# One-hots by group, one product for both fields: the placing step of a routed feed-forward on Trainium2

## What is computed

```python
def _L1_ffn_ref(x, Wr, br, ln_g, ln_b, W1, b1, W2, b2):
    TOP_K = 2
    xt = x.reshape(N, D)
    logits = xt @ Wr + br
    probs = jax.nn.softmax(logits, axis=-1)
    top_p, top_idx = jax.lax.top_k(probs, TOP_K)
    weights = top_p / top_p.sum(axis=-1, keepdims=True)
    ...
    xn = (xt - mu) * jax.lax.rsqrt(var + LN_EPS)
    xe = xn[None, :, :] * ln_g[:, None, :] + ln_b[:, None, :]
    h = jax.nn.gelu(jnp.einsum('end,edh->enh', xe, W1) + b1[:, None, :], approximate=False)
    y = jnp.einsum('enh,ehd->end', h, W2) + b2[:, None, :]
    ...
    out = (weights[:, :, None] * sel).sum(axis=1)
```

## Time and profile before

| | |
|---|---|
| median of 3 runs | 3544.34 us (3541.79 to 3544.54) |
| the profiled execution, its own time | 3536.91 us |
| span of the core in it | 3535.1 us |
| mean granted TensorE clock | 0.873 of full speed |
| TensorE busy | 2639.2 us (75%) in 15311 instructions |
| VectorE busy | 2619.7 us (74%) in 6603 |
| ScalarE busy | 1007.9 us (29%) in 2073 |
| GpSimd busy | 2179.5 us (62%) in 2147 |

### The profile page before, as it was taken

One profiled execution on the slowest core, in us unless ns is written; L12 is line 12 of the kernel. 1 busy time (PEld: TensorE's weight loads), 2 busy tenths in 40 slices (PEclk: granted clock), 3 DMA queues, 4 the chain that ended last, 5 costly groups with the idle time before them and its releaser, 6 DMA issues. The chain is left out here.

```text
span 3535.1 us, 55789 instructions
## 1 busy us (share of the span) xinstructions
PE 2639.2 (75%) x15311; PEld 2236.0 (63%) x15311; DVE 2619.7 (74%) x6603; ACT 1007.9 (29%) x2073; POOL 2179.5 (62%) x2147
## 2 busy tenths in 40 slices
PE   6888466666666665899956776777677569999997
PEld 4777354444444444789945555555555369999997
DVE  6999566666666666969967777777777778888886
ACT  0021000000000002545501111111111268888886
POOL 0455577777777774345567777777777235555554
PEclk9999677788788777999978888888888789999999
DMA  3011433333333332001133333333333447777775
GB/s 98 10 43 33 121 105 106 105 105 105 105 106 105 106 105 66 1 3 37 45 99 113 111 112 113 112 112 112 111 113 112 130 145 209 214 213 210 209 213 131
DMA packets 164679, 389.01 MB, mean 110 GB/s; under 512 B 46378, under 2 KB 95602, under 8 KB 151019
## 3 DMA queue, kind: packets, MB, share of 16 engines
q0 software_dynamic: 99072, 233.49, 24.5%
q1 hardware_dynamic: 65387, 152.94, 13.3%
HBM read 343.97 MB, written 42.98 MB: 109 GB/s over the span
## 5 line engine op out<-in xcount | busy, mean ns | idle before, releaser
L1081 POOL DMA_INDIRECT g_got<-table,e_source x1568 | 1492.0, 952 | 505.9 <-issue 458.2
L1174 PE MATMUL psum<-g_got,g_route 128*128 x3328 | 1082.0, 483 | 649.5 <-DMA g_got<-table,e_source 266.0
L1174 PEld LDWEIGHTS psum<-g_got,g_route 128*128 128x128 f32 x3328 | 760.4, 239 | 892.0 <-issue 766.9
L1107 DVE TENSOR_TENSOR A<-A,psum 128x256 f32 x1664 | 698.8, 420 | 525.7 <-PE psum L1174 347.4
L1090 DVE TENSOR_SCALAR g_route<-columns,e_local,e_weight 128x128 f32<-128x128 f32 x1664 | 471.1, 362 | 17.5 <-issue 12.5
L368 POOL DMA_INDIRECT records<-rec,place x120 | 149.6, 1247 | 220.4 <-ACT rec L580 122.2
L142 PE MATMUL psum<-e_xt_hi,e_w_hi 128*128 128x256 f32 x832 | 238.9, 287 | 34.3 <-DVE e_w_lo L1973 25.8
L1582 POOL TENSOR_TENSOR f_ht_lo<-f_ht,f_ht_hi 128x512 fp32r<-128x512 f32 x100 | 133.9, 1343 | 185.7 <-ACT f_ht_hi L1531 180.2
L142 PE MATMUL psum<-e_w_hi,e_ht_hi 128*128 128x256 f32 x832 | 237.5, 285 | 3.1 <-DVE e_w_lo L1981 3.1
L1860 POOL DMA_INDIRECT out<-e_y,e_homes x104 | 198.9, 1913 | 63.4 <-POOL e_homes L1856 47.6
L144 PE MATMUL psum<-e_xt_hi,e_w_lo 128*128 128x256 f32 x832 | 233.6, 281 | 0.0
(11 more groups left out here) (420 smaller groups left out, 5147.7 us busy)
## 6 DMA issues: line engine op xcount, KB each, us to landing
e_w<-in_m_w SPq DMA_DIRECT2D x104, 1024.0 KB, 5.3
g_got<-table,e_source POOLq DMA_INDIRECT x1568, 2.8
expert_table<-g_normal SPq DMA_DIRECT2D x52, 128.0 KB
table<-xn SPq DMA_DIRECT2D x49, 128.0 KB, 1.7
X<-in_x SPq DMA_DIRECT2D x1, 6144.0 KB
table<-f_ring SPq DMA_DIRECT2D x24, 256.0 KB, 2.1
out<-X SPq DMA_DIRECT2D x1, 6144.0 KB
f_w<-in_f_w SPq DMA_DIRECT2D x2, 1024.0 KB, 6.8
```

Of the source, the lines that this page charges most:

```text
L1081: pool.indirect_dma_start(got[:, c % RING, :], None, rows, bass.IndirectOffsetOnAxis(ap=source[:, c:c + 1].bitcast(U32), axis=0)).then_inc ...
L1107: dve.tensor_tensor(to, to, sums_of(c), ALU.add).then_inc(added, 1)
L1174: ins = pe.matmul(sums_of(c), route[:, c % (GB + GSEM), :], row(got, at[j % GSEM]), start=True, stop=True)
```

## The change

The one-hots of a group are written by one tensor_tensor each, from bf16 operands: the numbers 0 to 127, each repeated 14 times (`numbers_b`), against the 14 slots' `slot_hi` or `slot_lo`, now bf16 too. So the slots stand innermost: `is_hi` is [112, 14] and `is_lo` [128, 14] in a partition, where they were [14, 112] and [14, 128]. ScalarE reads `is_hi` across that order and writes `fields` as [14 slots, 2 fields, 112], each operation's output with its innermost dimension contiguous. One product of 224 columns for each slot then takes both fields, and its stationary operand, `is_lo[:, u, :, c]`, is read in steps of 14 elements. The two fields' sums, now side by side in bank 5, are added by VectorE before `node_of`.

Further: TensorE makes the totals of the experts with seven accumulating products of 112 columns, ahead of its others, and VectorE reduces their 14 x 8 numbers. `pick` is compared with the numbers less 8 (`lower`, made by GpSimd) instead of having 8 added. GpSimd waits for `node_of` behind its reading of the number of pairs instead of ahead of it. VectorE waits, before it writes the first low part of w1, until GpSimd has copied the second pair of nodes. `dense` and `second` share memory with `others` and `picked`.

```diff
-            dense, second = early("dense", [P, NT, NE]), early("second", [P, NT, NE])
+            dense, second = others, picked
...
-            is_lo = early("is_lo", [P, 2, 2 * GROUP, P], BF16)
-            is_hi = early("is_hi", [P, 2, 2 * GROUP, SC], BF16)
-            fields = here("fields", [P, 2, 2, 2 * GROUP, SC], BF16)
+            is_lo = early("is_lo", [P, 2, P, 2 * GROUP], BF16)
+            is_hi = early("is_hi", [P, 2, SC, 2 * GROUP], BF16)
+            fields = here("fields", [P, 2, 2 * GROUP, 2, SC], BF16)
+            numbers_b = early("numbers_b", [P, P, 2 * GROUP], BF16)
...
+                        if isinstance(m, int) and m == 0:
+                            pool.wait_ge(chosen, NODES)
                         wait(pool, x_ready, m - 1)
...
+                pool.tensor_scalar(lower[:], columns[:, 0:NE], -float(NE), None, ALU.add).then_inc(prepared, 1)
+                pool.tensor_copy(ones_b[:], ones[:]).then_inc(prepared, 1)
                 pool.tensor_copy(before_b[:], before[:]).then_inc(prepared, 1)
-                pool.tensor_copy(ones_b[:], ones[:]).then_inc(prepared, 1)
-                pool.tensor_copy(columns_b[:], columns[:]).then_inc(prepared, 1)
+                pool.tensor_copy(numbers_b[:], columns[:].unsqueeze(2).to_broadcast([P, P, 2 * GROUP])).then_inc(prepared, 1)
...
+                for q in range(GROUPS):
+                    ins = pe.matmul(psum[:, 6, 0:2 * GROUP * NE], ones_b[:], flat[:, q * 2 * GROUP * NE:(q + 1) * 2 * GROUP * NE],
+                                    start=q == 0, stop=q == GROUPS - 1)
+                ins.then_inc(ranked, 1)
...
-                    pe.wait_ge(fields_ready, 8 * g + 1)
-                    for c in range(2 * GROUP):
-                        pe.matmul(psum[:, 5, 0:SC], is_lo[:, u, c, :], fields[:, u, 0, c, :], start=opens and c == 0, stop=False)
                     for i in range(GROUP):
                         pe.wait_ge(fields_ready, 8 * g + (2 + i))
                         for c in (2 * i, 2 * i + 1):
-                            ins = pe.matmul(psum[:, 5, 0:SC], is_lo[:, u, c, :], fields[:, u, 1, c, :], start=False,
-                                            stop=closes and c == 2 * GROUP - 1)
+                            ins = pe.matmul(psum[:, 5, 0:2 * SC], is_lo[:, u, :, c], fields[:, u, c, :, :].rearrange("p f h -> p (f h)"),
+                                            start=opens and c == 0, stop=closes and c == 2 * GROUP - 1)
...
                         if isinstance(m, int) and m == 0:
+                            dve.wait_ge(nodes_ready, 2)
                             low_of_w1(m, u)
...
-                    s(dve.tensor_scalar(pick[:], pick[:], float(NE), None, ALU.add))
-                    s(dve.tensor_tensor(hot[:, :, k, :], numbers, wide(pick[:]), ALU.is_equal))
+                    s(dve.tensor_tensor(hot[:, :, k, :], lower[:].unsqueeze(1).to_broadcast([P, NT, NE]), wide(pick[:]), ALU.is_equal))
...
-                dve.tensor_reduce(count[:], hot[:].rearrange("p t k e -> p e (t k)"), AX.X, ALU.add).then_inc(chosen, 1)
...
+                s(dve.tensor_reduce(count[:], psum[:, 6, 0:2 * GROUP * NE].rearrange("p (c e) -> p e c", e=NE), AX.X, ALU.add))
...
-                    high_hots(g, u)
-                    for c in range(2 * GROUP):
-                        ins = dve.tensor_scalar(is_lo[:, u, c, :], columns_b[:], slot_lo[:, bass.ds(g * (2 * GROUP) + c, 1)], None, ALU.is_equal)
-                    ins.then_inc(hots_ready, 1)
+                    for to, of, wide, done in ((is_hi, slot_hi, SC, is_hi_ready), (is_lo, slot_lo, P, hots_ready)):
+                        dve.tensor_tensor(to[:, u, :, :], numbers_b[:, 0:wide, :],
+                                          of[:, bass.ts(g, 2 * GROUP)].unsqueeze(1).to_broadcast([P, wide, 2 * GROUP]),
+                                          ALU.is_equal).then_inc(done, 1)
...
-                dve.tensor_scalar(node_of[:], psum[:, 5, 0:SC], -1.0, 0.0, ALU.add, ALU.max).then_inc(chosen, 1)
+                s(dve.tensor_copy(pad[:], psum[:, 5, 0:SC]))
+                s(dve.tensor_tensor(number[:], pad[:], psum[:, 5, SC:2 * SC], ALU.add))
+                dve.tensor_scalar(node_of[:], number[:], -1.0, 0.0, ALU.add, ALU.max).then_inc(chosen, 1)
...
-                    act.activation(fields[:, u, 0, :, :].rearrange("p c h -> p (c h)"), is_hi[:, u, :, :].rearrange("p c h -> p (c h)"),
+                    act.activation(fields[:, u, :, 0, :], is_hi[:, u, :, :].rearrange("p h c -> p c h"),
                                    ACT.Copy, scale=part_1[:, 0:1]).then_inc(fields_ready, 1)
                     for i in range(GROUP):
-                        act.activation(fields[:, u, 1, 2 * i:2 * i + 2, :].rearrange("p c h -> p (c h)"),
-                                       is_hi[:, u, 2 * i:2 * i + 2, :].rearrange("p c h -> p (c h)"),
+                        act.activation(fields[:, u, 2 * i:2 * i + 2, 1, :], is_hi[:, u, :, 2 * i:2 * i + 2].rearrange("p h c -> p c h"),
                                        ACT.Copy, scale=float(P * (g * GROUP + i))).then_inc(fields_ready, 1)
```

More of the change, by code:

```diff
@@ L1767, in build @@
             slot_f, slot, slot_part = early("slot_f", [P, C]), early("slot", [P, C], I32), early("slot_part", [P, C], I32)
-            slot_lo, slot_hi = early("slot_lo", [P, C]), early("slot_hi", [P, C])
-            is_lo = early("is_lo", [P, 2, 2 * GROUP, P], BF16)
-            is_hi = early("is_hi", [P, 2, 2 * GROUP, SC], BF16)
-            fields = here("fields", [P, 2, 2, 2 * GROUP, SC], BF16)
-            columns_b, before_b, ones_b = (early(what, [P, P], BF16) for what in ("columns_b", "before_b", "ones_b"))
+            slot_lo, slot_hi = early("slot_lo", [P, C], BF16), early("slot_hi", [P, C], BF16)
+            is_lo = early("is_lo", [P, 2, P, 2 * GROUP], BF16)
+            is_hi = early("is_hi", [P, 2, SC, 2 * GROUP], BF16)
+            fields = here("fields", [P, 2, 2 * GROUP, 2, SC], BF16)
+            numbers_b = early("numbers_b", [P, P, 2 * GROUP], BF16)
+            before_b, ones_b = (early(what, [P, P], BF16) for what in ("before_b", "ones_b"))
+            lower = early("lower", [P, NE])
+            number = at[:].rearrange("p c e -> p (c e)")[:, 0:SC]
             part_1, pad, past_end = early("part_1", [P, 1]), early("pad", [P, SC]), early("past_end", [P, 2])
@@ L1941, in _ @@
                 halves = [flat[:, h * NT * NE:(h + 1) * NT * NE] for h in range(2)]
-                pe.wait_ge(prepared, 8)
+                pe.wait_ge(prepared, 9)
                 pe.wait_ge(chosen, CHOICES)
+                for q in range(GROUPS):
+                    ins = pe.matmul(psum[:, 6, 0:2 * GROUP * NE], ones_b[:], flat[:, q * 2 * GROUP * NE:(q + 1) * 2 * GROUP * NE],
+                                    start=q == 0, stop=q == GROUPS - 1)
+                ins.then_inc(ranked, 1)
                 for h in range(2):
                     pe.matmul(psum[:, 3 + h, 0:NT * NE], ones_b[:], halves[h], start=True, stop=True).then_inc(ranked, 1)
-                pe.wait_ge(chosen, COUNT)
-                pe.matmul(psum[:, 6, 0:NE], ones[:], count[:], start=True, stop=True).then_inc(ranked, 1)
                 for h in range(2):
@@ L2043, in _ @@
                 dve.tensor_tensor(behind[:], top[:, :, 1], top[:, :, 0], ALU.subtract).then_inc(chosen, 1)
-                dve.tensor_reduce(count[:], hot[:].rearrange("p t k e -> p e (t k)"), AX.X, ALU.add).then_inc(chosen, 1)
-                for h in range(2):
-                    dve.wait_ge(ranked, h + 1)
-                    s(dve.tensor_copy(sums[:, :, 1 + h * NT:1 + (h + 1) * NT],
-                                      psum[:, 3 + h, 0:NT * NE].rearrange("p (c e) -> p e c", e=NE)))
                 dve.wait_ge(ranked, TOTALLED)
-                s(dve.tensor_scalar(ntile_i[:], psum[:, 6, 0:NE], float(MT - 1), None, ALU.add))
+                s(dve.tensor_reduce(count[:], psum[:, 6, 0:2 * GROUP * NE].rearrange("p (c e) -> p e c", e=NE), AX.X, ALU.add))
+                s(dve.tensor_scalar(ntile_i[:], count[:], float(MT - 1), None, ALU.add))
                 s(dve.tensor_scalar(ntile_i[:], ntile_i[:], 8, None, ALU.logical_shift_right))
@@ L2055, in _ @@
                 s(dve.tensor_scalar(sums[:, :, 0], first[:], float(MT), None, ALU.mult))
-                dve.wait_ge(prepared, 8)
+                for h in range(2):
+                    dve.wait_ge(ranked, COUNTED + h)
+                    s(dve.tensor_copy(sums[:, :, 1 + h * NT:1 + (h + 1) * NT],
+                                      psum[:, 3 + h, 0:NT * NE].rearrange("p (c e) -> p e c", e=NE)))
+                dve.wait_ge(prepared, 9)
                 s(dve.tensor_tensor_scan(upto[:].rearrange("p e c -> p (e c)"), keep[:].rearrange("p e c -> p (e c)"),
@@ L2070, in _ @@
                 s(dve.tensor_copy(slot_hi[:], slot_part[:]))
-                def high_hots(g, u):
-                    for c in range(2 * GROUP):
```

(2 more changed lines are left out.)

15 lines of the change are left out of this document (7 added, 8 removed).

## The result

| | before | after |
|---|---|---|
| median, same chip | 3541.28 us (3536.1 to 3547.21, 11 runs) | 3549.07 us (3546.67 to 3557.78, 11 runs) |
| ratio, 95% interval | | 1.0022 (1.0013 to 1.0031) |
| span of the profiled execution | 3535.1 us | 3544.8 us |
| choices begin | 2797.99 | 2799.50 |
| first expert product | 2864.11 | 2876.75 |

The account below looks back on a forecast made before the run. VectorE's one-hots filled the stretch before; ScalarE's strided field reads were to bound it after. +10.0 up to node_of, + 0.6 - 0.9 - 0.8 = +8.9 us on 3544.3 made 3553.2 us; range 3531 to 3555.

Parts of the forecast that it names:

- Fields on ScalarE: Fields of each group: ScalarE's reads 28 bytes apart cost 1.75 ns an element, making a group 6.42 us instead of 3.56.
- Rival 3: ScalarE's scattered read pays an addition, 1.55 ns an element: +4.5 us, 3548.8; chance 0.52 together with the forecast's own case.
- Rivals 1 and 2: Fields at ScalarE's old pace: 3533.4 us (chance 0.33); with VectorE's bf16 one-hots at one element a cycle: 3537.6 us (0.07).
- One-hots: VectorE's two one-hot operations a group take 1.0 + 1.1 us; is_hi's earlier readiness is worth -1.4 us.
- Product and weights: TensorE's 14 products a group, 2.6 us, or 3.1 by strided weight loads, run beside ScalarE; the last pair adds 0.6.
- End: From last products to first expert product: two added VectorE operations +0.6, GpSimd's wait -0.9, second gather -0.8; together -1.1 us.
- Start: Choice of experts: each of two searches loses one tensor_scalar of 0.19 us, -0.4 us; GpSimd's constants cost nothing.
- hidden, with the dearer copy barely: GpSimd's nine constant steps, done by 2803.1 to 2805.3, cost nothing, as TensorE wants them at 2805.3.
- The counts: Totals of the experts, from the last one-hot to the scan: 3.7 us against 4.0, taken as -0.1.
- Rounds: Expert rounds behind the first expert product: a chain of their own, shifting by what that product shifts, +8.9 us.
- the prediction's own sign: The prediction is wrong if ScalarE's durations don't grow, and if the expert rounds don't keep their distance from the first product.

Follow-up runs that it names:

- p1: The changed kernel plus seven ScalarE copies of 448 f32 elements, read 4 to 64 bytes apart, in idle time: 577 ns at 4 bytes, 997 at 16.
- e1: The changed kernel with ScalarE reading is_hi in memory order and node numbers made by a formula: 3931.73 us beside 3945.56 of before, ratio 0.9956.
- e5: The kernel before with only GpSimd's wait for node_of moved behind its reading of the number of pairs: ratio to before 0.9996.
- e6: The kernel before with only VectorE's added wait for the second pair of nodes, ahead of its first low part of w1: ratio to before 0.9984.
- e3: The changed kernel with numbers_b made by ScalarE instead of GpSimd: 3554.60 us in a single run; choices to first expert product 75.86 us for 77.25.
- e4: The kernel before with both of the change's waits, GpSimd's for node_of and VectorE's for the second pair of nodes: ratio to before 0.9981.
- e8: The kernel before with one already met wait added on VectorE where it idles, ahead of its wait for the last placing products: ratio to before 0.9987.
- v1: The changed kernel with is_hi slot by slot again, by one tensor_tensor a group, and ScalarE reading and writing in order: ratio to before 0.9966.
- v2: v1 with numbers_b made by ScalarE instead of GpSimd: 3531.46 us beside 3543.64 of before, ratio 0.9964.
- e2: The changed kernel with ScalarE reading is_hi as it lies and writing fields across, 448 bytes apart: 4007.67 us beside 3945.56 of before, ratio 1.0157.
- e7: The kernel before with two already met waits, on GpSimd and VectorE, in the places of those of e4: ratio to before 0.9984.

## Why the prediction was right, and where its steps failed

The forecast was 3553.2 us, +8.9 on the median shown, slower; measured was +7.8, to 3549.07 us (the median of before is 3541.28 over the 11 runs, 3.1 below that of the three shown). By its steps:

- **Fields on ScalarE: right.** Expected were 3.0 and 0.58 us a piece and a period of 6.42; measured 3.11, 0.59 and 6.52. The pace read from two VectorE rows at 16 and 396 bytes, 1.75 ns, holds for ScalarE at 28 bytes: p1 gives 1.78, and e1 that all of it hangs on the read. The term was sized 0.9 us too small, +11.9 for +12.8 from the first fields to the steps of node_of, of which seven periods of 0.1 us are 0.7. Rival 3, the addition at 1.55 ns, is excluded by the 16-byte copy, which would have taken 0.90 us and took 1.00. Rivals 1 and 2 fell with the durations.
- **One-hots: right.** 975 and 1085 ns for the estimates of 1.0 and 1.1, with half the time an element of the rows it was taken from. is_hi was ready 1.3 us earlier for the 1.4 said.
- **Product and weights: right.** 14 products in 3.60 us beside ScalarE's 3.59, and weights in steps of 28 bytes load in 150 ns on the mean, unseen beside the products.
- **End: right.** +0.56 for the added steps (said +0.6), and node_of's end to the first product 9.09 us for 10.73, -1.64 (said -1.7). e5 and e6 show what the prediction's sum hid: the -0.9 for GpSimd is there only with VectorE's wait; the two terms don't add up from separate edits.
- **Start: wrong.** The step that failed is "hidden, with the dearer copy barely". The price of the copy was right (1.68 us, the cheap end of 1.7 to 3.9), and TensorE indeed didn't wait for it. But it was weighed only against who waits for its result, not against who runs beside it: it stretched L2037 by 1.37 us, and waiting for `lower` took 0.22. The choices got 1.0 us longer where 0.4 shorter was said. e3 shows the cause. The counts behind them were right: from the last one-hot to the scan 3.8 us for 4.0, where -0.1 was taken.
- **Rounds: wrong.** "A chain of their own, which I expect to shift by what this point shifts" held only to within 2.9 us; by the prediction's own sign ("if the expert rounds don't keep their distance from the first product") this step failed. By the fifth tile after was 0.87 us behind, then each of 47 tiles was 0.071 shorter, -3.3, and the last steps gave 0.4. The 0.87 go with the clock: over the first 46 us behind the first expert product the granted clock was 0.89 in before and 0.86 in after. e4 puts 0.055 of the 0.071 down to one more instruction on VectorE (e6 to e8, on other chips, 0.03 to 0.04 against before's trace, 0.06 to 0.07 against e5's); the rest, 0.01 to 0.02 a tile, is open. So +11.1 in the stretch became +8.2, and the forecast of +8.9 was nearly met because a missed +1.4, a term 0.9 too small and a missed -2.9 cancelled. The mechanism, ScalarE's read as the new bound, was right; the closeness of the number is partly luck.

## What to carry to other kernels

When an edit changes an access pattern so that one engine reads or writes more densely, price the other engine that uses the same tensor by its new stride. Here one-hots at double pace on VectorE turned ScalarE's read into one new 16-byte piece per element, and the engine with 0.93 us to spare became the bound. The layout that is slower for VectorE and in order for ScalarE (v1, v2) was faster than before, where the change was slower. Ask of any work moved to GpSimd which VectorE instruction stands beside it, not only who waits for it. And take a difference of under 0.1% in a long loop for noise of code and clock until a control with an idle instruction shows otherwise.

## What the runs showed of the hardware that was not expected

- ScalarE's read of SBUF costs 1.78 ns for each new piece of 16 bytes in f32 (p1) and 1.80 in bf16 (after), and two elements a piece are nearly enough to hide it (611 for 577 ns).
- A scattered bf16 write costs ScalarE 5.1 ns an element (e2), 2.6 times the time of the scattered read.
- A single tensor_tensor of 392 elements took 1.94 us for 0.57 beside a GpSimd copy of 1792 (after), and 1.92 in v1 with another kind of operation; a gather of GpSimd was stretched from 1.0 to 2.8 us by VectorE's 2.29 (e5).
- One instruction more on VectorE, without effect of its own, changed 0.515 us of issue time a tile to 0.458 (e8), or 47 x 0.057 = 2.7 us over the rounds.
- The instant at which TensorE's clock rises varied between otherwise equal stretches. The last products of the placing took 1.2 and 1.3 us longer with it (e6, e8), and the first tiles of the rounds 1.5 and 1.3 (e7, e8).
